# A graph network on one core: transfers with other outer row counts, and four accumulation tables instead of eight

## The chip, the cores and the metric

The kernel runs on one core of one Trainium2 chip. The metric is the device time of one execution in microseconds (us), the median of the runs shown. A core has five instruction streams: TensorE (PE, with its weight loads PEld), VectorE (DVE), ScalarE (ACT), GpSimd (POOL) and SyncE (SP), which here only issues transfers. 16 DMA engines move the data between HBM and the on-chip memory (SBUF).

## The reference

Two message-passing layers on a graph of 6250 nodes and 206250 directed edges, 128 features, float32. Both normalise first and add their result to `x`.

```
h = relu(layernorm(x))
# layer 0: graph convolution, with self loops added
deg  = segment_sum(w, src); dinv = rsqrt(deg)
x   += relu(segment_sum(dinv[src] * w * dinv[dst] * (h @ kernel)[dst], src) + bias)
h = relu(layernorm(x))
# layer 1: messages along each edge in both directions, mean over them
fwd  = concat([h[src], edge_attr]) @ W_fwd + b_fwd      # summed at dst
back = concat([h[dst], edge_attr]) @ W_back + b_back    # summed at src
agg  = (segment_sum(fwd, dst) + segment_sum(back, src)) / count
x   += gamma * layernorm(leaky_relu(agg) + h) + beta
```

The edges come sorted by `dst`.

## The kernel before

The program is a row of blocks, one after the other; between two blocks all engines meet. What matters of each:

**Setup** (`setup_and_degrees`, L86 to L368). SP loads `src`, `dst` and the weights as 128 partitions of 1616 edges. 206250 edges fill 127 such rows (`ROWFULL`), and one row has 1018. Then `x` comes in as 125 partitions (`NP`) of 50 nodes. DVE starts its own work when the three edge arrays are there (L248), turns them into tables of node rows and columns, and then makes one-hot tables for 101 steps of 16 times 128 edges, which PE multiplies into counts and degrees (L300 to L320, L354). Its last instruction (L337) scales `x` by the inverse root of the degree and lets SP store it as `g` (L186). Meanwhile SP stores the padded edge arrays (L166), loads them again in groups (L170), and makes `near` (L172): a table in HBM of `NEAR` = 51563 rows of 64 floats, row r being the 64 keys from edge 4r on. Next SP fills the accumulation tables with zeros (L178), ten transfers of 640 KB for each of the `K` = 8 tables. All these are queued on SP in the order of the code. The block ends when all of them have landed.

**Edge pass** (`edge_pass`, name `gw`). 202 groups of 8 times 128 edges. PE builds the message rows with one-hot matrices, ACT copies them to SBUF, and POOL adds each chunk of 128 rows to an HBM table with one indirect DMA (L497), table `j % K` for chunk `j` of the group. Ahead of a chunk POOL waits until the last add to the same table has landed (L495).

**Node update** (`gcn_nodes`). Nodes are again 125 partitions of 50. SP loads `g` and the left half of the columns of all `K` tables, in two halves of 25 nodes a partition (L710), into three buffers; DVE adds them up (L813). Queued behind the first three loads on SP is a small load of node counts (L721), which DVE needs (L769) to find rows of `near`; POOL then gathers 50 tiles of them (L744), and DVE (L801) turns them into the places that the next block uses. DVE's order is: the row numbers, the sum of half 0, its products (L820, L824), the places, the sum of half 1, its products. At the end SP stores `x1` and `h1`.

**Counts times features** (`dense_sums`). 25 steps (`t`), in each of which DVE makes one-hot tables (L1077, L1078), PE makes count matrices of them and multiplies them with the features, and ACT and DVE take the results away. Beside it POOL adds up the right half of the columns of the `K` tables (L1052), one half table in each of the steps 2 to 2K - 1.

**Last update** (`last_nodes`). Loads of `h1` and `x1` as 125 partitions (L1370, L1371), 50 small products with bias, activation and normalisation, and two stores of half the output (L1374).

Of the kernel before, what the change touches and what calls it, by code (L numbers as in the profile page):

```python
# [53 lines left out]
K = 8  # L54
# [6 lines left out]
NEAR = E // STEP + 1  # L61
# [5 lines left out]
ROUND = 12582912.0  # L67

# [21 lines left out]
def setup_and_degrees(nc, d):  # L90
# [4 lines left out]
    with ExitStack() as ctx:  # L95
# [58 lines left out]
        @block.sync  # L154
        def _(sp):

            sp.wait_ge(pads, 3)
            for a, t in ((d.src, src_i), (d.dst, dst_i), (d.w, w_run)):
                sp.dma_start(t[0:ROWFULL, :], a[0:ROWFULL * EC].rearrange("(p c) -> p c", c=EC)).then_inc(edges_in, 16)
                sp.dma_start(t[ROWFULL:ROWFULL + 1, 0:ROWTAIL], a[ROWFULL * EC:E].rearrange("(p c) -> p c", p=1)).then_inc(edges_in, 16)  # L160
            sp.dma_start(x[:], d.x.rearrange("(p t) f -> p t f", p=NP)).then_inc(x_in, 16)
# [24 lines left out]
            sp.dma_start(d.g[0:N, :].rearrange("(p t) f -> p t f", p=NP), x[:]).then_inc(stored, 16)  # L186
            sp.wait_ge(stored, 16 * 4)
            sp.wait_ge(cleared, 16 * (CUT * K + 2))
# [18 lines left out]
        def _(act):  # L207

            act.wait_ge(x_in, 16)
# [18 lines left out]
        def _(dve):  # L228
# [19 lines left out]
            dve.wait_ge(edges_in, 16 * 6)  # L248
# [399 lines left out]
def gcn_nodes(nc, d):  # L648
# [4 lines left out]
    with ExitStack() as ctx:  # L653
# [51 lines left out]
        def _(sp):  # L705
            def load_part(n):
                r, k = divmod(n, K)
                if n >= PB:
                    sp.wait_ge(part_used, n - PB + 1)
                sp.dma_start(part[:, n % PB, :, :], half(nodes(d.tab_gcn[k]), r)[:, :, 0:F]).then_inc(part_in[n % PB], 16)  # L710

            sp.dma_start(d.count_dst.rearrange("(p t) -> p t", p=NP), d.cnt_dst[:]).then_inc(cnt_stored, 16)
            for at, t in ((0, one), (1, next_one)):
                sp.dma_start(t[:], d.dst_f[at:at + E].rearrange("(p c) -> p c", p=NP)).then_inc(dst_in, 16)
            sp.dma_start(half(acc, 0), half(nodes(d.g), 0)).then_inc(acc_in[0], 16)
# [11 lines left out]
            sp.dma_start(x[:], nodes(d.x)).then_inc(x_in, 16)  # L727
            sp.dma_start(half(acc, 1), half(nodes(d.g), 1)).then_inc(acc_in[1], 16)
# [4 lines left out]
            sp.dma_start(nodes(d.x1), x[:]).then_inc(stored, 16)  # L733
            for r in range(2):
                sp.wait_ge(h_ready, HT * (r + 1))
                sp.dma_start(half(nodes(d.h1), r), half(acc, r)).then_inc(stored, 16)
            sp.wait_ge(stored, 16 * 4)
# [11 lines left out]
        def _(dve):  # L749
# [8 lines left out]
            def starts():  # L758
# [4 lines left out]
                dve.wait_ge(dst_in, 32)  # L763
# [45 lines left out]
            def add_up(r):  # L809
                dve.wait_ge(acc_in[r], 16)  # L810
                for n in range(r * K, (r + 1) * K):
                    dve.wait_ge(part_in[n % PB], 16 * (n // PB + 1))
# [20 lines left out]
            dve.wait_ge(x_in, 16)  # L833
# [85 lines left out]
def dense_sums(nc, d):  # L919
# [7 lines left out]
    with ExitStack() as ctx:  # L927
# [70 lines left out]
        def _(sp):  # L998
# [5 lines left out]
            def store(i, h, first, last):  # L1004
                t = 2 * i + h
                if isinstance(i, int) and i == 0:
                    sp.dma_start(d.src_attr_half(h), d.table_half(0, h)).then_inc(acc_in[h], 16)
                elif isinstance(i, int) and i < K:
                    if i >= 2:
                        sp.wait_ge(part_used, 2 * (i - 2) + h + 1)  # L1010
                    sp.dma_start(d.part_half(h), d.table_half(i, h)).then_inc(part_in[h], 16)
# [13 lines left out]
        def _(pool):  # L1025
# [10 lines left out]
            def take(i, h, first, last):  # L1036
# [10 lines left out]
                if isinstance(i, int) and 1 <= i < K:  # L1047
                    pool.wait_ge(acc_in[h], 16)
                    pool.wait_ge(part_in[h], 16 * i)
# [279 lines left out]
def last_nodes(nc, d):  # L1329
# [3 lines left out]
    with ExitStack() as ctx:  # L1333
# [30 lines left out]
        def _(sp):  # L1364
# [5 lines left out]
            sp.dma_start(h1[:], nodes(d.h1)).then_inc(h1_in, 16)  # L1370
            sp.dma_start(x1[:], nodes(d.x1)).then_inc(x1_in, 16)  # L1371
# [3 lines left out]
            sp.wait_ge(stored, 32)  # L1375

        @block.gpsimd
        def _(pool):

            pool.wait_ge(w_in, 16 * 8)  # L1380
            pool.wait_ge(x1_in, 16)
# [3 lines left out]
        def _(dve):  # L1385
# [17 lines left out]
            for r in range(2):  # L1403
                for t in range(r * HT, (r + 1) * HT):
# [8 lines left out]
                    if t == 0:  # L1413
                        dve.wait_ge(h1_in, 16)
# [157 lines left out]
```

## Time and profile before

| | |
|---|---|
| median of 3 runs | 6291.11 us (6288.08 to 6294.46) |
| profiled execution, its own time | 6287.51 us |
| its span in the trace | 6285.7 us |
| busy: PE, DVE, POOL, ACT | 57%, 48%, 48%, 30% of the span |
| bytes moved | 622.18 MB, 99 GB/s over the span |

No engine is busy for much more than half of the span, so the kernel has to be read block by block: setup from 0 to 1128.7 us, edge pass to 4390.4, node update to 4815, counts times features to about 6094, last update to the end. In the views below a time in brackets, as `[14.31 <-DMA ...]`, is how long the engine had stood idle before the instruction and what ended that. "DMA share" is how busy the 16 DMA engines are together: 0.06 is one engine at work all the time, 1.0 is all sixteen.

### The profile page before, as it was taken

The page shows a single profiled execution, that of the slowest core. Times are in us where ns is not written, and L with a number is a line of the kernel's source. Part 1 is how long each engine was busy: PE and PEld are TensorE (multiplying, and loading weights), DVE is VectorE, ACT ScalarE, POOL GpSimd, SP SyncE. Part 2 cuts the span into 40 slices and gives each one's busy share as a digit, 9 for nine tenths or more (in the row PEclk, how much of TensorE's full clock was granted, in tenths as well). Part 3 has the DMA queues.
Part 4 walks back from the last instruction along what each step waited for, and adds up shares of the span by engine and source line. Part 5 has one row for each costly group of instructions (what it writes and reads, how often), then busy time and mean ns, then how long its engine had stood idle before and what let it go on. Part 6 is the DMA issues. An engine that isn't in the chain of part 4 may idle for free. (4 is left out here: it accounts for less than half of the span.)

```text
span 6285.7 us, 93695 instructions
## 1 busy us (share of the span) xinstructions
PE 3579.1 (57%) x27946; PEld 3167.1 (50%) x28096; DVE 3009.3 (48%) x4263; ACT 1906.9 (30%) x5027; POOL 2993.7 (48%) x1727
## 2 busy tenths in 40 slices
PE   0555000566666666666666666664012988888984
PEld 0444000565666556665566555664011766666764
DVE  3999000444444444444444444443134656565536
ACT  1011000333333333333333333332013545455532
POOL 0000000688888888888888888887301011110000
PEclk9777555777777777777777777776555999999997
DMA  3300029677777777777777777776333111110011
GB/s 74 24 18 18 18 98 273 141 137 137 133 134 137 137 135 134 136 137 137 135 133 137 137 137 134 134 137 109 100 103 110 35 35 35 35 35 25 5 36 54
DMA packets 687907, 622.18 MB, mean 99 GB/s; under 512 B 252021, under 2 KB 595789, under 8 KB 685852
## 3 DMA queue, kind: packets, MB, share of 16 engines
q0 software_dynamic: 234304, 213.56, 28.8%
q1 hardware_dynamic: 453432, 406.13, 22.2%
q8 instruction: 133, 2.18, 0.1%
q14 instruction: 38, 0.31, 0.0%
HBM read 327.05 MB, written 305.66 MB: 101 GB/s over the span
## 5 line engine op out<-in xcount | busy, mean ns | idle before, releaser
L497 POOL DMA_INDIRECT gcn_sums<-gw_sums,gw_to_i x1616 | 2750.8, 1702 | 1490.3 <-ACT gw_sums L643 1003.5
L581 PE MATMUL bank<-gw_window,gw_spread_hot 128*128 128x128 f32 x3232 | 793.4, 349 | 1291.4 <-DVE gw_spread_hot L539 1290.4
L581 PEld LDWEIGHTS bank<-gw_window,gw_spread_hot 128*128 128x128 f32 x3232 | 642.5, 255 | 1329.0 <-issue 809.3
L643 ACT COPY gw_sums<-bank 128x256 f32<-128x256 f32 x1616 | 601.9, 372 | 1465.6 <-PE bank L606 1169.8
L600 PE MATMUL bank<-gw_sum_hot,gw_attrs 128*128 128x128 f32 x3232 | 795.4, 336 | 395.5 <-DVE gw_sum_hot L543 198.0
L633 ACT ACTIVATE gw_pay<-bank,gw_rec 128x128 f32<-128x128 f32 x1616 | 593.5, 370 | 1160.2 <-PE bank L581 1139.6
L600 PEld LDWEIGHTS bank<-gw_sum_hot,gw_attrs 128*128 128x128 f32 x3232 | 629.1, 242 | 444.3 <-issue 444.3
L604 PE MATMUL bank<-gw_pay,gw_same 128*128 128x128 f32 x3232 | 757.1, 323 | 2.7 <-ACT gw_pay L633 2.6
L561 DVE CAST gw_to_i<-gw_to_f 128x8 int32<-128x8 f32 x202 | 34.9, 173 | 1481.2 <-DMA gcn_sums<-gw_sums,gw_to_i 1481.1
L606 PE MATMUL bank<-gw_attrs,gw_same 128*128 128x128 f32 x3232 | 744.0, 318 | 0.0
L604 PEld LDWEIGHTS bank<-gw_pay,gw_same 128*128 128x128 f32 x3232 | 625.8, 241 | 3.6 <-ACT gw_pay L633 2.9
L606 PEld LDWEIGHTS bank<-gw_attrs,gw_same 128*128 128x128 f32 x3232 | 613.3, 236 | 0.0
L1154 PE MATMUL bank<-ds_counts,ds_parts 128*128 128x256 bf16 x3675 | 597.3, 278 | 0.0
L539 DVE TENSOR_SCALAR gw_spread_hot<-gw_rel_b,part 128x1024 f32<-128x1024 bf16 x202 | 230.4, 1141 | 532.1 <-DMA gw_rel_b<-dst_offset 504.5
L354 PE MATMUL bank<-places,row_hot 128*128 128x200 bf16 x1616 | 269.6, 293 | 339.6 <-DVE places L307 339.6
L1199 ACT COPY ds_turned<-bank 128x1024 bf16<-128x1024 bf16 (+1 forms) x325 | 311.5, 963 | 470.3 <-PE bank L1140 470.3
L1103 DVE TENSOR_TENSOR src_sums<-src_sums,bank 128x512 f32<-128x512 f32 (+1 forms) x325 | 211.3, 656 | 485.4 <-PE bank L1170 481.3
L1170 PE MATMUL bank<-ds_turned,ds_now 128*128 128x512 bf16 (+1 forms) x1800 | 435.0, 377 | 10.0 <-issue 2.8
L1052 POOL TENSOR_TENSOR src_attr<-src_attr,attr_by_dst 125x3200 f32<-125x3200 f32 x14 | 102.0, 7285 | 623.3 <-issue 519.7
L541 DVE TENSOR_TENSOR gw_same<-gw_key_b,gw_rec 128x1024 f32<-128x1024 int16 x202 | 397.2, 1966 | 0.0
L354 PEld LDWEIGHTS bank<-places,row_hot 128*128 128x128 bf16 x1616 | 195.2, 121 | 372.4 <-DVE places L307 360.4
L1183 ACT CAST ds_counts<-bank 128x392 bf16<-128x392 f32 x800 | 344.5, 502 | 122.4 <-PE bank L1120 122.0
(199 smaller groups left out, 4793.7 us busy)
## 6 DMA issues: line engine op xcount, KB each, us to landing
gw_attrs<-in_edge_attr SPq DMA_DIRECT2D x201, 512.0 KB
gw_rel_b<-dst_offset SPq DMA_DIRECT2D x202, 256.0 KB, 4.0
gw_key_b<-src_key SPq DMA_DIRECT2D x202, 256.0 KB
gcn_sums<-zeros SPq DMA_DIRECT2D x80, 640.0 KB
gcn_sums<-gw_sums,gw_to_i POOLq DMA_INDIRECT x1616, 3.8
n_part<-gcn_sums SPq DMA_DIRECT2D x16, 1562.5 KB
attr_by_dst<-gcn_sums SPq DMA_DIRECT2D x14, 1562.5 KB
gw_window<-g SPq DMA_DIRECT2D x202, 64.0 KB, 4.0
```

Of the source, the lines that this page charges most:

```text
L354: nc.tensor.matmul(hist[:, 0:4 * NT], row_hot[:, h, 0, j, :], col_w[:, h, j, :, :].rearrange("p s n -> p (s n)"), **ends)
L497: nc.gpsimd.indirect_dma_start(out=tables[j % K], out_offset=bass.IndirectOffsetOnAxis(ap=to_i[:, h, j:j + 1], axis=0), in_=sums[:, h, j, ...
L541: nc.vector.tensor_tensor(same[:, h, :, :], by_chunk(key_b), per_edge(key_row), ALU.is_equal).then_inc(same_ready, 1)
L581: nc.tensor.matmul(row_bank[j % 2][:, 0:F], spread_hot[:, h, j, :], window[:, h, :], start=True, stop=True).then_inc(row_ready, 1)
L600: nc.tensor.matmul(win_bank[h][:, 0:P], attrs[:, h, j, :], sum_hot[:, h, j, :], **ends)
L604: last = nc.tensor.matmul(bank[j % B][:, 0:F], same[:, h, j, :], pay[:, h, j, :], start=True, stop=True)
L606: last = nc.tensor.matmul(bank[j % B][:, F:2 * F], same[:, h, j, :], attrs[:, h, j, :], start=True, stop=True)
L633: nc.scalar.activation(pay[:, h, j, :], row, ACT.Copy, scale=rec[:, h, 3, j:j + 1]).then_inc(paid, 1)
L643: nc.scalar.copy(sums[:, h, j, :], bank[j % B][:, 0:width]).then_inc(staged, 1)
L1154: ins = nc.tensor.matmul(row_bank[:, 0:2 * P], parts[:, tile, s, :], counts[:, h, tile, :, :].rearrange("p b q -> p (b q)"), start=(tile = ...
L1170: ins = nc.tensor.matmul(back_bank[v][:, 0:n], now[:, h, half, s, :], turned[:, v, half, 0:n], start=(half == 0 and s == 0), stop=(half == ...
L1183: nc.scalar.copy(to, pair_bank[batch % B][:, 0:PB * HH].rearrange("p (c k) -> p k c", c=PB)).then_inc(pair_copied, 1)
```

## The change

The number of tables `K` goes from 8 to 4. Every transfer over 125 partitions in the places shown is cut into one of 120 and one of 5, and the three edge loads of 127 partitions into one of 112 and one of 15. `near` has 51568 rows instead of 51563, the next multiple of 16. The semaphore counts follow. (Broadcast loads of 125 partitions and the 128-partition transfers are as they were.)

```diff
-K = 8
+K = 4
-NEAR = E // STEP + 1
+NEAR = 16 * -(-(E // STEP + 1) // 16)
+NODE_CUTS = (slice(0, 120), slice(120, NP))
+EDGE_CUTS = (slice(0, 112), slice(112, ROWFULL))
...
-                sp.dma_start(t[0:ROWFULL, :], a[0:ROWFULL * EC].rearrange("(p c) -> p c", c=EC)).then_inc(edges_in, 16)
+                rows = a[0:ROWFULL * EC].rearrange("(p c) -> p c", c=EC)
+                for cut in EDGE_CUTS:
+                    sp.dma_start(t[cut, :], rows[cut, :]).then_inc(edges_in, 16)
...
-            sp.dma_start(d.g[0:N, :].rearrange("(p t) f -> p t f", p=NP), x[:]).then_inc(stored, 16)
+            for cut in NODE_CUTS:
+                sp.dma_start(d.g[0:N, :].rearrange("(p t) f -> p t f", p=NP)[cut], x[cut]).then_inc(stored, 16)
...
-                sp.dma_start(part[:, n % PB, :, :], half(nodes(d.tab_gcn[k]), r)[:, :, 0:F]).then_inc(part_in[n % PB], 16)
+                for cut in NODE_CUTS:
+                    sp.dma_start(part[cut, n % PB, :, :], half(nodes(d.tab_gcn[k]), r)[cut, :, 0:F]).then_inc(part_in[n % PB], 16)
...
-            sp.dma_start(h1[:], nodes(d.h1)).then_inc(h1_in, 16)
+            for cut in NODE_CUTS:
+                sp.dma_start(h1[cut], nodes(d.h1)[cut]).then_inc(h1_in, 16)
...
-                sp.dma_start(half(nodes(d.out), 1 - r), half(agg, 1 - r)).then_inc(stored, 16)
+                for cut in NODE_CUTS:
+                    sp.dma_start(half(nodes(d.out), 1 - r)[cut], half(agg, 1 - r)[cut]).then_inc(stored, 16)
```

The same cut stands at the loads of `x` (twice), the two key arrays `one` and `next_one`, `g` (both halves), the half tables in `dense_sums`, and `x1`, and at the stores of `x1` and `h1`.

On SP, in setup before, from the last padded array's reload to the end of the block's transfers, with the number of rows behind each:

```order
L170 DMA rec<-w_pad 128x202x8
L172 DMA near<-src_float 51563x64
L178 DMA gcn_sums<-zeros 128x1280 [waits setup_zeroed]
L178 DMA gcn_sums<-zeros 128x1280 x79
L180 DMA g<-zeros 75x256
L180 DMA h<-zeros 75x256
L183 DMA dst_offset<-rel 128x202x8 [waits setup_rec_ready]
L184 DMA edge_records<-rec 128x202x32
L186 DMA g<-x_sb 125x6400 [waits setup_g_ready]
```

And in the changed kernel, whose lines are numbered a little higher:

```order
L175 DMA rec<-w_pad 128x202x8
L177 DMA near<-src_float 51568x64
L183 DMA gcn_sums<-zeros 128x1280 [waits setup_zeroed]
L183 DMA gcn_sums<-zeros 128x1280 x39
L185 DMA g<-zeros 75x256
L185 DMA h<-zeros 75x256
L188 DMA dst_offset<-rel 128x202x8 [waits setup_rec_ready]
L189 DMA edge_records<-rec 128x202x32
L192 DMA g<-x_sb 120x6400 [waits setup_g_ready]
L192 DMA g<-x_sb 5x6400
```

The order is the same; 40 of the 80 fills are gone, and the store of `g` is two transfers.

On POOL, in the edge pass's loop, the first five indirect adds of a group before. The names of the waits are those of the first block that used the semaphore: `setup_normed` is here ACT's "chunk is in SBUF", `setup_g_ready` the group's row numbers, and `setup_step`, `setup_stored`, `setup_cleared` and `gw_added3`, `gw_added4` the landing of adds to tables 0, 1, 2, 3 and 4:

```order
L493 ISA [waits setup_g_ready]
L495 REGISTER_ALU [waits setup_normed]
L497 DMA gcn_sums<-gw_sums,gw_to_i 6400x256 [waits setup_step]
L493 REGISTER_ALU
L497 DMA gcn_sums<-gw_sums,gw_to_i 6400x256 [waits setup_normed,setup_stored]
L493 REGISTER_ALU
L497 DMA gcn_sums<-gw_sums,gw_to_i 6400x256 [waits setup_normed,setup_cleared]
L493 REGISTER_ALU
L497 DMA gcn_sums<-gw_sums,gw_to_i 6400x256 [waits setup_normed,gw_added3]
L493 REGISTER_ALU
L497 DMA gcn_sums<-gw_sums,gw_to_i 6400x256 [waits setup_normed,gw_added4]
```

The same five in the changed kernel:

```order
L499 ISA [waits setup_g_ready]
L501 ISA [waits setup_normed]
L503 DMA gcn_sums<-gw_sums,gw_to_i 6400x256 [waits setup_step]
L499 REGISTER_ALU
L503 DMA gcn_sums<-gw_sums,gw_to_i 6400x256 [waits setup_normed,setup_stored]
L499 REGISTER_ALU
L503 DMA gcn_sums<-gw_sums,gw_to_i 6400x256 [waits setup_normed,setup_cleared]
L499 REGISTER_ALU
L503 DMA gcn_sums<-gw_sums,gw_to_i 6400x256 [waits setup_normed,gw_added3]
L499 REGISTER_ALU
L501 ISA [waits setup_normed]
L503 DMA gcn_sums<-gw_sums,gw_to_i 6400x256 [waits setup_step]
```

The fifth add goes to table 0 again and waits for the first add of the same group, four adds back, where before each waited for the one eight back. One register instruction more stands in each group.

On SP, at the start of the node update before (the wait ahead of L721 is for the store of the counts):

```order
L712 DMA count_dst<-cnt_dst 125x50
L714 DMA n_one<-dst_float 125x1650
L714 DMA n_next_one<-dst_float 125x1650
L715 DMA n_acc<-g 125x3200
L710 DMA n_part<-gcn_sums 125x25x128 x3
L721 DMA n_cnt_tp<-count_dst 48x128 [waits setup_hot_used,setup_mean_ready]
L722 DMA n_cnt_tp<-count_dst 1x106
L710 DMA n_part<-gcn_sums 125x25x128 [waits setup_runs_ready] x5
L725 DMA n_w<-in_L_gnn_kernel 128x128
L726 DMA n_bias<-in_L_gnn_bias 125x128
L727 DMA n_x<-in_x 125x6400
```

In the changed kernel, from the third half table on:

```order
L717 DMA n_part<-gcn_sums 120x25x128
L717 DMA n_part<-gcn_sums 5x25x128
L730 DMA n_cnt_tp<-count_dst 48x128 [waits setup_hot_used,setup_mean_ready]
L731 DMA n_cnt_tp<-count_dst 1x106
L717 DMA n_part<-gcn_sums 120x25x128 [waits setup_runs_ready]
L717 DMA n_part<-gcn_sums 5x25x128
L734 DMA n_w<-in_L_gnn_kernel 128x128
L735 DMA n_bias<-in_L_gnn_bias 125x128
L737 DMA n_x<-in_x 120x6400
L737 DMA n_x<-in_x 5x6400
```

One half table instead of five stands between the counts and `x`.

## Rows read from the trace of the kernel before

**Rows 1.** Windows of setup: us, busy us (instructions) of each engine, TensorE clock, DMA share, GB/s.
```profile
20.00:30.00 10.00, 0.00 (x0) 0.00 (x0) 0.00 (x0) 0.00 (x0) 0.00 (x0) 1.00 0.06 27
200.00:300.00 100.00, 56.67 (x680) 49.67 (x678) 100.00 (x150) 0.00 (x0) 0.00 (x0) 0.77 0.08 18
930.00:940.00 10.00, 0.00 (x0) 0.00 (x0) 0.00 (x0) 0.00 (x0) 0.00 (x0) 0.50 1.02 411
1115.00:1120.00 5.00, 0.00 (x0) 0.00 (x0) 0.00 (x0) 0.00 (x0) 0.00 (x0) 0.50 0.30 128
```

**Rows 2.** Timeline of SP's issues in setup and at the edge pass's start: start, us.
```profile
168.22 14.96 SPq L172 DMA_DIRECT2D near<-src_float  x1
183.22 840.77 SPq L178 DMA_DIRECT2D gcn_sums<-zeros  x80
...
1078.90 22.60 SPq L186 DMA_DIRECT2D g<-x_sb  x1
1128.68 0.38 SPq L448 DMA_DIRECT2D gw_rec<-edge_records  x1
```

**Rows 3.** Timeline of DVE in setup: its first conversion and its last instruction.
```profile
102.69 1.00 DVE L249 CAST attr_sums<-src_i 128x1616 f32<-128x1616 int32 x1 [99.30 <-DMA attr_sums<-in_edge_weight]
623.63 6.82 DVE L337 TENSOR_TENSOR x_sb<-x_sb,dinv 125x6400 f32<-125x6400 f32 x1
```

**Rows 4.** The indirect adds of L497 in the edge pass.
```profile
L497 POOL DMA_INDIRECT gcn_sums<-gw_sums,gw_to_i x1616: 1543/1547/2832, 1141.0 to 4383.1; - x180
...
DMA to landing us min/median/max: 3.6/3.8/7.9
```

**Rows 5.** Timeline of POOL there, the first add of a group.
```profile
2006.66 1.55 POOL L497 DMA_INDIRECT gcn_sums<-gw_sums,gw_to_i  x1 [0.30 <-DMA gcn_sums<-gw_sums,gw_to_i]
```

**Rows 6.** Timeline of SP: node update's first and last issues, next block's first.
```profile
4390.44 0.26 SPq L712 DMA_DIRECT2D count_dst<-cnt_dst  x1
...
4784.63 9.86 SPq L736 DMA_DIRECT2D h<-n_acc  x2
4815.22 7.56 SPq L1001 DMA_DIRECT2D src_sums<-h  x5
```

**Rows 7.** Timeline of DVE in the node update.
```profile
4470.64 0.28 DVE L769 TENSOR_REDUCE n_tile_cnt<-n_cnt_tp 50x1 f32<-50x128 f32 x1 [58.93 <-DMA n_cnt_tp<-count_dst]
4476.09 10.54 DVE L813 TENSOR_TENSOR n_acc<-n_acc,n_part 125x3200 f32<-125x3200 f32 x3
...
4595.85 0.35 DVE L820 SCALAR_TENSOR_TENSOR n_scaled<-bank,dinv,n_bias 125x128 f32<-125x128 f32 x1 [21.68 <-DMA n_x<-in_x]
...
4743.06 3.49 DVE L813 TENSOR_TENSOR n_acc<-n_acc,n_part 125x3200 f32<-125x3200 f32 x1 [13.37 <-DMA n_part<-gcn_sums]
```

**Rows 8.** Timeline of POOL there: the first, second and last of 50 gathers.
```profile
4474.99 1.01 POOL L744 DMA_INDIRECT n_near<-near,n_near_row_i  x1 [90.30 <-POOLq L742]
4476.30 4.13 POOL L744 DMA_INDIRECT n_near<-near,n_near_row_i  x1 [0.30 <-issue]
...
4551.58 0.94 POOL L744 DMA_INDIRECT n_near<-near,n_near_row_i  x1 [0.30 <-issue]
```

**Rows 9.** POOL's adds of half tables, L1052, all 14.
```profile
L1052 POOL TENSOR_TENSOR src_attr<-src_attr,attr_by_dst x14: 6959/7134/7875, 4976.1 to 5652.5; 125x3200 f32<-125x3200 f32 x14
```

**Rows 10.** Timeline of POOL: one add, and two copies of later steps.
```profile
5444.34 7.76 POOL L1052 TENSOR_TENSOR src_attr<-src_attr,attr_by_dst 125x3200 f32<-125x3200 f32 x1 [44.27 <-issue]
...
5735.93 0.83 POOL L1046 COPY ds_now<-ds_parts 128x768 bf16 x1 [52.48 <-PE bank L1170]
...
6009.99 0.83 POOL L1046 COPY ds_now<-ds_parts 128x768 bf16<-128x768 bf16 x1 [47.57 <-PE bank L1170]
```

**Rows 11.** Timeline of DVE beside that add.
```profile
5445.22 7.71 DVE L1078 TENSOR_TENSOR ds_hi_hot<-ds_numbers,ds_twos 128x1568 bf16<-128x1568 bf16 x1
```

**Rows 12.** Timeline of DVE in the last update: first use of `h1`, last instruction.
```profile
6146.14 0.35 DVE L1415 SCALAR_TENSOR_TENSOR n_agg<-n_leaky,n_per_count,n_h 125x128 f32<-125x128 f32 x1 [22.51 <-DMA n_h<-h]
...
6262.45 3.49 DVE L1437 TENSOR_TENSOR n_agg<-n_agg,n_x 125x3200 f32<-125x3200 f32 x1
```

More of the change, by code:

```diff
@@ L207, in _ @@
         def _(act):
-            act.wait_ge(x_in, 16)
+            act.wait_ge(x_in, 32)
             for t in range(NT):
@@ L709, in load_part @@
                     sp.wait_ge(part_used, n - PB + 1)
-                sp.dma_start(part[:, n % PB, :, :], half(nodes(d.tab_gcn[k]), r)[:, :, 0:F]).then_inc(part_in[n % PB], 16)
+                for cut in NODE_CUTS:
+                    sp.dma_start(part[cut, n % PB, :, :], half(nodes(d.tab_gcn[k]), r)[cut, :, 0:F]).then_inc(part_in[n % PB], 16)
             sp.dma_start(d.count_dst.rearrange("(p t) -> p t", p=NP), d.cnt_dst[:]).then_inc(cnt_stored, 16)
             for at, t in ((0, one), (1, next_one)):
-                sp.dma_start(t[:], d.dst_f[at:at + E].rearrange("(p c) -> p c", p=NP)).then_inc(dst_in, 16)
-            sp.dma_start(half(acc, 0), half(nodes(d.g), 0)).then_inc(acc_in[0], 16)
+                for cut in NODE_CUTS:
+                    sp.dma_start(t[cut, :], d.dst_f[at:at + E].rearrange("(p c) -> p c", p=NP)[cut, :]).then_inc(dst_in, 16)
+            for cut in NODE_CUTS:
+                sp.dma_start(half(acc, 0)[cut], half(nodes(d.g), 0)[cut]).then_inc(acc_in[0], 16)
             for n in range(PB):
@@ L726, in _ @@
             sp.dma_start(bias[:], d.bias.rearrange("(o f) -> o f", o=1).to_broadcast([NP, F])).then_inc(w_in, 16)
-            sp.dma_start(x[:], nodes(d.x)).then_inc(x_in, 16)
-            sp.dma_start(half(acc, 1), half(nodes(d.g), 1)).then_inc(acc_in[1], 16)
+            for cut in NODE_CUTS:
+                sp.dma_start(x[cut], nodes(d.x)[cut]).then_inc(x_in, 16)
+            for cut in NODE_CUTS:
+                sp.dma_start(half(acc, 1)[cut], half(nodes(d.g), 1)[cut]).then_inc(acc_in[1], 16)
             for n in range(K, 2 * K):
@@ L732, in _ @@
             sp.wait_ge(x1_ready, NT)
-            sp.dma_start(nodes(d.x1), x[:]).then_inc(stored, 16)
+            for cut in NODE_CUTS:
+                sp.dma_start(nodes(d.x1)[cut], x[cut]).then_inc(stored, 16)
             for r in range(2):
                 sp.wait_ge(h_ready, HT * (r + 1))
-                sp.dma_start(half(nodes(d.h1), r), half(acc, r)).then_inc(stored, 16)
-            sp.wait_ge(stored, 16 * 4)
+                for cut in NODE_CUTS:
+                    sp.dma_start(half(nodes(d.h1), r)[cut], half(acc, r)[cut]).then_inc(stored, 16)
+            sp.wait_ge(stored, 16 * 7)
         @block.gpsimd
@@ L832, in _ @@
             dve.wait_ge(w_in, 32)
-            dve.wait_ge(x_in, 16)
+            dve.wait_ge(x_in, 32)
             products(0)
@@ L1006, in store @@
                 if isinstance(i, int) and i == 0:
-                    sp.dma_start(d.src_attr_half(h), d.table_half(0, h)).then_inc(acc_in[h], 16)
+                    for cut in NODE_CUTS:
+                        sp.dma_start(d.src_attr_half(h)[cut], d.table_half(0, h)[cut]).then_inc(acc_in[h], 16)
                 elif isinstance(i, int) and i < K:
@@ L1010, in store @@
                         sp.wait_ge(part_used, 2 * (i - 2) + h + 1)
-                    sp.dma_start(d.part_half(h), d.table_half(i, h)).then_inc(part_in[h], 16)
+                    for cut in NODE_CUTS:
+                        sp.dma_start(d.part_half(h)[cut], d.table_half(i, h)[cut]).then_inc(part_in[h], 16)
                 elif isinstance(i, int) and i == K and h == 0:
@@ L1047, in take @@
                 if isinstance(i, int) and 1 <= i < K:
-                    pool.wait_ge(acc_in[h], 16)
-                    pool.wait_ge(part_in[h], 16 * i)
+                    pool.wait_ge(acc_in[h], 32)
+                    pool.wait_ge(part_in[h], 32 * i)
                     if i >= 2:
@@ L1369, in _ @@
             sp.dma_start(row_sums[:], d.row_t[:, 0:N]).then_inc(row_in, 16)
-            sp.dma_start(h1[:], nodes(d.h1)).then_inc(h1_in, 16)
-            sp.dma_start(x1[:], nodes(d.x1)).then_inc(x1_in, 16)
+            for cut in NODE_CUTS:
+                sp.dma_start(h1[cut], nodes(d.h1)[cut]).then_inc(h1_in, 16)
+            for cut in NODE_CUTS:
+                sp.dma_start(x1[cut], nodes(d.x1)[cut]).then_inc(x1_in, 16)
             for r in range(2):
                 sp.wait_ge(out_ready, r + 1)
-                sp.dma_start(half(nodes(d.out), 1 - r), half(agg, 1 - r)).then_inc(stored, 16)
-            sp.wait_ge(stored, 32)
+                for cut in NODE_CUTS:
+                    sp.dma_start(half(nodes(d.out), 1 - r)[cut], half(agg, 1 - r)[cut]).then_inc(stored, 16)
+            sp.wait_ge(stored, 64)
         @block.gpsimd
```

16 lines of the change are left out of this document (8 added, 8 removed).

## The prediction

> **What bounds the kernel now.** I read the windows of setup first, then SP's timeline, then DVE's and POOL's, block by block.
>
> The windows show how many DMA engines a transfer uses [rows 1]. With the 127-row edge loads alone in flight the share is 0.06 and the rate 27 GB/s: one engine of 16. The 125-row store of `g` has 0.30 and 128 GB/s, five engines at 25.6. The 128-row fills have 1.02 and 411 GB/s, sixteen at 25.7. From 200 to 300 us there are 18 GB/s at 0.08 (one engine, and a little for bookkeeping): that is `near`, in 256-byte pieces. 127 is prime, 125 has 5, 128 has 16, and 51563 has no divisor from 2 to 16. So the count that decides is the largest divisor up to 16 of the outer rows.
>
> Four places pay for it. Setup: DVE idles 99.3 us for the edges, then works until 630.45 [rows 3]; `near` holds the queue, the fills behind it take until about 1040, two small stores and `g` follow, and the edge pass starts at 1128.68 [rows 2]. Node update: DVE waits for half tables, `x` and the counts [rows 7]. The last update waits for `h1` [rows 12] and for its stores. The edge pass is another matter: 1616 indirect adds in 3242 us from first to last start are 2.006 us each, of which the add is 1.55 or more and a gap 0.30 [rows 4, 5]; POOL is never still, so it sets the pace there.
>
> **Edge loads.** The three arrays are 2.46 MB, by one engine at 26 GB/s 95 us. With 112 + 15 rows the most loaded engine has 8 rows of 6464 bytes and the tail, 56 KB for each array, 167 KB, 6.4 us. 102.69 was 2.8 (first issue) + 94 of data + 6 of rest, so DVE starts near 15.4: **-87**. DVE's 527.8 us from there to its end are its own work (100.00 of 100 us busy from 200 to 300 [rows 1]), so they only move: 630.45 becomes 543.
>
> **`near`, fills, small stores.** Sixteen engines at 18 GB/s copy 13.2 MB in 46 us; on one engine it stays 733. Issue comes at 168 - 87 = 81. Half the fills, 26.2 MB at 411 GB/s, are 64 us, and the small stores at most 55 (from the last fill's issue, 183.22 + 840.77 = 1024, to 1078.90 [rows 2]). Together 165 us, over by about 246; DVE works until 543. So the cover left is some 300 us: `near` could take 340 us and cost nothing. Without DVE's cover this part would cost the 165. The halved fills are worth nothing by themselves.
>
> **Store of `g`.** From the end of its issue, 1101.5, to 1128.68 are 27.2 us [rows 2], 25 of them data. Fifteen engines have 8 rows, five of them one more: 9 of 25.6 KB at 25.6 GB/s are 9 us. With a second issue 12 us. The edge pass starts at 543 + 12 = 555 instead of 1128.7: **-574** for setup.
>
> **Edge pass.** An add now waits for the one four back, started 8.0 us before; landing takes 3.8 us in the middle and 7.9 at most [rows 4]. So it costs nothing: below that it could only gain if fewer tables made an add faster, for which no row speaks. The extra register instruction per group: before a group's first add two more stand than before the others, and its gap is the same 0.30 [rows 5]. Bounds 0 and 0.06 us x 202 = 12 us; I take 0. 3261.7 us as before, and the node update starts at 3817.
>
> **Node update**, counted from its first issue; before, 424.8 us [rows 6]. A half table takes 13.37 + 3.49 = 16.9 us on five engines [rows 7], where each moves 625 pieces of 512 bytes, 27 ns a piece; now the fullest moves 225, **6.1 us**. The bounds are 6.1 and 16.9.
> - Keys 4.5, `g` 4.4, three half tables 18.3, start and landing 4.3: the counts come at 31.5, not 80.2.
> - DVE's row numbers take 4.35 until POOL's first gather [rows 7, 8]: 35.9. The 50 gathers took 77.5 us, 1.25 each and more beside one of DVE's adds (4.13 against 0.94 [rows 8]). 6 adds gave 15 us; now 4 adds and 3 similar operations fall there, 17.5: 80 us, and 3.6 landing: 119.5. **POOL's gathers are next to be late**; they were hidden.
> - Meanwhile DVE: three adds to 47.5, the fourth to 53, `x` (9 us instead of 25) at 59, products to 75, three operations for the places to 85, then a wait of 34 us for the gathers.
> - The places end 12.5 later, 132. Four adds, the last waiting for its buffer, to 147.6; ACT is then still busy with squares of half 0, for which I allow 2 us: 149.5.
> - From the last add's end, 4746.55, the block took 68.7 us [rows 6, 7]. Of these 20.7 stand behind the issue of the last store of `h1` (4794.49), which queues behind 4.8 MB more on the same five engines. With its own 4.4 us of data, 9.2 are left: 57.2. Sum 206.7: **-218**.
>
> **Counts times features.** While POOL adds (7.76 us), a DVE operation that lasts 0.97 elsewhere takes 7.71 [rows 10, 11], and PE then waits for its one-hots. A step with an add is (5652.5 - 4976.1) / 13 = 52.0 us [rows 9]; without one (6009.99 - 5735.93) / 6 = 45.7 [rows 10]. Eight adds fewer (14 to 6) at 6.3: **-50**. The bounds are 0, and 8 x 7.8 = 62.
>
> The Trainium skill (SBUF — State Buffer, Who interferes with whom) says that a VectorE instruction with two SBUF inputs and a GpSimd one that reads SBUF block each other fully. By that rule each add costs at most its own length, 8 x 7.1 = 57; by the steps of the trace it is 50. The trace agrees.
>
> **Last update.** `h1` on five engines is 24.4 us of data, on fifteen 8.8: -16. POOL's addition to `x1` and its collision with DVE stay. The two stores run from 6259 to the end; after DVE's end at 6265.94 [rows 12] 19.8 us are left, now 4.4 of data and 3 of start and end: -12. **-28**.
>
> **Sum.** 574 + 218 + 50 + 28 = 870. The profiled execution had 6287.5 (span 6285.7), 3.6 under the median 6291.1; so 5417 on its scale, and **5420** as a median.
>
> **The rivals.**
>
> *The scatter chain becomes the bound.* Two adds to one table are now four apart. If an add had to wait, the step is a quarter of the landing time. For it: the largest landing seen, 7.9 us, is only 0.1 under 8.0. Against: the middle is 3.8. At 8.5 us it costs 0.12 x 1616 = 190 and gives 5610. The sum of 870 is used up at (2.006 + 0.54) x 4 = 10.2 us landing; above that, at 10.7, the time is 6490 and the kernel slower. Chance 4%, and 1% for slower.
>
> *`near` stays on one engine* (if the copy's other side decides). It then starts at 81, ends at 814, fills to 878, small stores to 933, `g` to 945, 390 later than 555: 5810. Against it: the 128-row fills do use all. 3%.
>
> *The cut pieces do not run wider.* The Trainium skill (DMA: Bandwidth & Descriptors, Rules for kernel authors) advises against two transfers for two parts of the partitions, since both go through the same sixteen engines anyway. As a mechanism of this kernel: the edge loads keep 87, `g` 14, the last update 28, and the half tables stay at 16.9 us, so that the counts come at 80 and the node update takes about 277, 71 more. 5420 + 87 + 14 + 28 + 71 = 5620. Against it: the whole transfers of 127 and 125 rows used one and five engines [rows 1], so there is something to widen. The same page (Why a DMA increments its semaphore by 16 and not by 1) says that the largest divisor up to 16 decides. 5%.
>
> *Only a smaller thing is off*: instruction delivery, the gathers, clock, 30 to 70 us either way, inside the range.
>
> **How the numbers follow.** Forecast 86%, scatter chain 5%, `near` 3%, no wider 5%, other 1%. The range is made of the forecast's own terms: below, 50 us if gathers and half tables run freer than I take them and the adds cost 62; above, 12 for the register instruction, 1% of the edge pass (33), and 25 for the node update: 5370 to 5490. Within 0.2%, or 12.6 us of 6291, a measurement tells nothing from no change; faster 0.98, same 0.005, slower 0.015.
>
> **What the changed profile would show.** DVE's first conversion near 15 us; DMA share near 1 while `near` is copied, and no stretch at 18 GB/s; the edge pass starting at 555, with an add every 2.006 us and gaps of 0.30; the counts about 31 us after the node update's first issue, then DVE idle some 34 us until the gathers have landed; 6 adds of L1067, and long operations at the line of the one-hots only beside them; `h1` 16 us earlier. Wrong it would be by gaps on POOL that end with the landing of an add, by a window of 18 GB/s, or by half tables 17 us apart.

## The result

The changed kernel took 5476.8 us (median, 5471.4 to 5481.0), the kernel before 6290.6 beside it: 0.8706, 95% interval 0.8694 to 0.8718. The forecast was 5420, range 5370 to 5490. The time lies in the range and 57 us above the forecast. The profiled execution took 5479.9 (span 5478.1), and its forecast was 5417. The blocks, each from its first DMA issue to the next block's, divide the span and so nearly all of the difference.

| block, us | before | forecast | changed |
|---|---|---|---|
| setup | 1128.7 | 555 | 565.2 |
| edge pass | 3261.8 | 3262 | 3277.4 |
| node update | 424.8 | 207 | 226.1 |
| counts times features | 1281.9 | 1232 | 1227.7 |
| last update | 188.6 | 161 | 181.6 |

SP's issues in setup and at the edge pass's start, in the timeline of the changed kernel (start, us):

```profile
76.03 14.25 SPq L177 DMA_DIRECT2D near<-src_float  x1
90.33 101.27 SPq L183 DMA_DIRECT2D gcn_sums<-zeros  x40
...
543.03 0.70 SPq L192 DMA_DIRECT2D g<-x_sb  x2
565.20 0.37 SPq L454 DMA_DIRECT2D gw_rec<-edge_records  x1
```

`near` and the 40 fills are issued by 192 us, in place of 1024 [rows 2], and their data are through by about 207; no stretch at 18 GB/s and a share of 0.08 is left. DVE's last instruction of setup ends at 543.0, as forecast, and sets the store of `g`. But from there the edge pass is 22.2 us away, not 12. The windows of the changed kernel (columns as in [rows 1]) say why:

```profile
120.00:140.00 20.00, 12.44 (x152) 10.92 (x148) 20.00 (x30) 0.00 (x0) 0.00 (x0) 0.74 1.18 262
205.00:220.00 15.00, 8.01 (x110) 7.15 (x107) 15.00 (x24) 0.00 (x0) 0.00 (x0) 0.86 0.13 47
545.00:547.00 2.00, 0.00 (x0) 0.00 (x0) 0.00 (x0) 0.00 (x0) 0.00 (x0) 0.50 0.94 205
3864.00:3868.00 4.00, 0.00 (x0) 0.00 (x0) 0.00 (x0) 0.00 (x0) 0.00 (x0) 0.50 1.12 183
```

The first row is the copy of `near`. The third is `g`'s 120 rows. The share of 0.94 is the fifteen engines that the reshaping was to give, yet they move 205 GB/s, 13.7 each, where five moved 25.6 each and sixteen 25.7 [rows 1]. The fourth row is the half tables of the node update: all engines busy, 183 GB/s. **A share near 1 isn't a rate near the top; the last column has to be read beside it.**

The edge pass, by its line (least, middle and longest ns; first and last start), and two places of POOL's timeline:

```profile
L503 POOL DMA_INDIRECT gcn_sums<-gw_sums,gw_to_i x1616: 1542/1547/3742, 577.5 to 3833.1; - x180
```
```profile
639.60 1.54 POOL L503 DMA_INDIRECT gcn_sums<-gw_sums,gw_to_i  x1 [0.30 <-issue]
641.96 1.55 POOL L503 DMA_INDIRECT gcn_sums<-gw_sums,gw_to_i  x1 [0.82 <-DMA gcn_sums<-gw_sums,gw_to_i]
```

First to last start is 3255.6 us, against 3242.1 [rows 4]. The second add waited 0.82 us for an earlier add to land. Of the 1615 gaps 29 are over 0.335 us, and they hold 11.2 us more than 0.30 each would; before there was none. The semaphore times of the trace say when each add landed: in 25 of the 29 the late add starts 0.76 to 0.78 us after the landing of the one four back, and no add of the pass starts sooner than 0.76 after it. 24 of the 29 are the seventh add of a group, which waits for the third.

DVE and POOL in the node update, in the timeline of the changed kernel:

```profile
3889.80 0.28 DVE L782 TENSOR_REDUCE n_tile_cnt<-n_cnt_tp 50x1 f32<-50x128 f32 x1 [31.90 <-DMA n_cnt_tp<-count_dst]
...
3977.07 1.83 DVE L814 TENSOR_SCALAR n_hi<-n_near 128x3200 f32<-128x3200 f32 x1 [16.81 <-DMA n_near<-near,n_near_row_i]
...
4005.28 3.49 DVE L826 TENSOR_TENSOR n_acc<-n_acc,n_part 125x3200 f32<-125x3200 f32 x1 [5.16 <-DMA n_part<-gcn_sums]
```
```profile
3894.16 1.01 POOL L757 DMA_INDIRECT n_near<-near,n_near_row_i  x1 [59.49 <-DVE n_near_row_i L792]
```

Counted from the block's first issue at 3842.64, the counts are there at 47.2 (forecast 31.5), the gathers have landed at 134.4 (119.5), the last add starts at 162.6. The late counts carry 16 of the block's 19 us: from the counts to the landed gathers it is 87.2 us, forecast 88.0. What comes after is 91.7, forecast 87.2; 3.5 of those 4.5 us are the last add, which waited 5.16 us for its half table; the forecast had 1.6 for it.

Counts times features has six adds of half tables, as forecast, and each is a little shorter than before (6.96 us in the middle, 7.13 in [rows 9]):

```profile
L1067 POOL TENSOR_TENSOR src_attr<-src_attr,attr_by_dst x6: 6959/6962/6967, 4222.8 to 4483.6; 125x3200 f32<-125x3200 f32 x6
```

The last update, in the timelines of PE (the first product with `row_sums`) and DVE (first use of `h1`, last instruction); the block begins at 5296.46:

```profile
5331.40 0.80 PE L1477 MATMUL bank<-n_w,n_row_sums 128*125 128x128 f32 x2 [13.51 <-DMA n_row_sums<-row_sums_t]
```
```profile
5347.39 0.35 DVE L1433 SCALAR_TENSOR_TENSOR n_agg<-n_leaky,n_per_count,n_h 125x128 f32<-125x128 f32 x1 [13.57 <-DMA n_h<-h]
...
5464.08 3.49 DVE L1455 TENSOR_TENSOR n_agg<-n_agg,n_x 125x3200 f32<-125x3200 f32 x1
```

`h1` is first used 50.9 us after the block's start, against 49.0 before [rows 12]; it was to come 16 us earlier. From DVE's end, 5467.57, to the span's end are 10.5 us, in place of 19.8: the stores did become shorter, by 9.3 of the forecast 12.

### The profile page after: what moved, and what is told of

It reads as the page before. It is cut to its first block and busy times, and to the rows that moved or that the text cites. A ratio compares the mean times of both kernels' runs of the same rounds, so it can differ in the third digit from the quotient of the medians.

```text
span 5478.1 us, 93494 instructions
## 1 busy us (share of the span) xinstructions
PE 3562.1 (65%) x27946; PEld 3159.2 (58%) x28096; DVE 2931.5 (54%) x4255; ACT 1898.5 (35%) x5027; POOL 2932.3 (54%) x1719
## 5 line engine op out<-in xcount | busy, mean ns | idle before, releaser
L1061 POOL COPY ds_now<-ds_parts 128x768 bf16 (+1 forms) x25 | 28.0, 1119 | 770.9 <-PE bank L1185 770.9
L1135 PE MATMUL bank<-ds_hi_hot,ds_lo_hot 128*128 128x98 bf16 x3200 | 282.7, 214 | 101.6 <-DVE ds_hi_hot L1093 101.6
```

## The experiments

A ratio is to the kernel before, timed on the same chip; a time without one is one execution.

**The terms one by one.**

*near_only*: the kernel before with a round row count for `near` alone.
```diff
-NEAR = E // STEP + 1
+NEAR = 16 * -(-(E // STEP + 1) // 16)
```

> The kernel before with 51568 rows in near and nothing else. If the copy then runs on all engines and DVE's work covers it with the fills and small stores, the edge pass starts at DVE's end plus the five-engine store of g, 630 + 27 = 658 instead of 1129, and the time is about 5820. If the copy stays on one engine, no change: 6290. In the changed kernel the fills and near overlapped and the whole queue was empty by about 207, so I expect the first. Edge pass, node update and last update as before.

Measured 5824.2 us; setup 659.0, the other blocks as before to within 5 us. `near` alone is 466 of the 814 us gained.

*k4_only*: the kernel before with four tables.
```diff
-K = 8
+K = 4
```

> The kernel before with four tables and nothing else. If the prediction's terms are separable: half the fills stand behind the one-engine copy of near, so setup loses 64 us (26.2 MB at 411 GB/s); the half tables stay at 16.9 us each but are half as many, the counts still come at 80 us, the node update falls from 425 to about 280; the steps with a POOL add fall from 14 to 6, -52; the last update stays. Sum 6030. What it is to tell: whether the edge pass is longer with four tables (3277 us as in the changed kernel, against 3262) with everything else as before. If four tables are the cause, 3275 or more here and a time near 6043; if the earlier start or the other transfers are, 3262.

Measured 6068.4 us. Setup 1064.5 (half the fills, with `near` still in front of them), node update 292.2 (with 21 us of pauses that are told of under x1_later), counts times features 1227.6 (-54); but the edge pass 3282.4 in place of 3261.8, and the last update, in which nothing differs, 199.8 in place of 188.6.

*all_but_k*: the changed kernel with eight tables.
```diff
-K = 4
+K = 8
```

> The changed kernel with eight tables again. If four tables cost the edge pass some 13 us (a few gaps on POOL above 0.30), it falls from 3277 to about 3262 here; if not, it stays. Node update: four more half tables on each side, of which the second half's adds (4 x 3.5) and the wait for their buffers show, about +30; the steps with an add go from 6 to 14, +52. Time about 5545 with the first, 5560 with the second.

Measured 5579.6 us (5576.7 to 5587.7), ratio 0.8869 [0.8854, 0.8884], 103 more than the changed kernel. Setup is the same, 564.9: the fills are hidden at either number. Node update 294.5, counts times features 1271.7, edge pass 3265.0. So four tables are worth 68 and 44 us in two blocks and cost 12 in a third. The adds of the edge pass by their line, with eight tables:

```profile
L503 POOL DMA_INDIRECT gcn_sums<-gw_sums,gw_to_i x1616: 1544/1548/3869, 576.9 to 3822.8; - x180
```

3245.9 us from first to last start. With eight tables the edge pass took 3261.8 to 3265.8 in three kernels, with four 3277.4 to 3290.3 in ten. No kernel of one kind reaches into the other: **the four tables cost the edge pass 12 to 29 us**. Long gaps there are none in the three, and 29 to 52 in each of the ten.

*k2*: the changed kernel with two tables, the loads of later half tables begun where the first three end.
```diff
-K = 4
+K = 2
```
```diff
-            for n in range(K, 2 * K):
+            for n in range(max(K, PB), 2 * K):
```

> The changed kernel with two tables: an add waits for the one two back, started 4.0 us before. Shown so far is 3.8 us from issue to landing, but not whether the issue is counted from the instruction's start or from its end, 1.55 us later. Counted from the start, a table's cycle is 3.8 + 0.3 = 4.1 us, 2.05 for an add, and the edge pass is some 70 us longer; with 26 us less in the steps with POOL adds and some 15 less in the node update the time is about 5505. Counted from the end, the cycle is 1.55 + 3.8 + 0.3 = 5.65, 2.83 for an add, the edge pass about 4570 us long, and the time about 6730. The second would also put the limit of four tables nearer: 5.65 of 8.0 us.

Measured 6377.6 us, slower than the kernel before; the edge pass takes 4186.9. The adds by their line:

```profile
L503 POOL DMA_INDIRECT gcn_sums<-gw_sums,gw_to_i x1616: 1542/1546/3806, 580.0 to 4746.3; - x180
```

The add itself is as long as ever (1546 ns), but an add starts only every 4166.3 / 1615 = 2.58 us, and two to one table 5.16 apart. That is the mean round trip of an add on one table. By the semaphore times, of which this trace lacks some, 1254 of 1614 adds start 0.76 to 0.80 us after the landing of the one before on their table, and a landing takes at least 4.3 us on average from the add's start. The 3.8 of [rows 4] was too short, because that line of the view counts 808 of the 1616 adds only: the tables 0, 5, 6 and 7, for whose landings the records are complete. By all semaphore times of the kernel before, the adds to table 2 take 6.2 us in the middle and 8.5 at the longest. The rival's mechanism exists; at four tables the room is 8.0 us on average against 5.16.

**The halved rate.** The store of `g` was half as fast as its engines. One theory: what counts is where the rows lie that the engines move at the same moment, and 15 engines with 8 rows each are a bad pattern. The other: something shared, or the number 15, limits any such transfer.

*cut112*:
```diff
-NODE_CUTS = (slice(0, 120), slice(120, NP))
+NODE_CUTS = (slice(0, 112), slice(112, NP))
```

> The changed kernel with the node rows cut into 112 + 13 instead of 120 + 5. In the changed kernel the 120-row transfers kept fifteen engines busy (share 0.90 to 0.96) at only 192 to 205 GB/s, 13 GB/s each, where five engines had 25.6 each. Theory A (where the rows lie): fifteen engines of eight neighbouring rows meet at the same part of SBUF and each runs at half speed; seven rows each on sixteen engines lie staggered, and the edge loads, cut so, had up to 290. Then g needs some 11 us of data instead of 18, the counts come near 38 instead of 47, and the time falls by 20 to 40 to about 5447. Theory B (a limit of the path to HBM for such rows, whatever the cut): still 200 GB/s and 5477. Theory C (the second, small piece is what costs, since it comes after the first): thirteen rows on thirteen engines instead of five on five, nearly the same, 5475.

Measured 5468.4 us (5465.1 to 5472.9), ratio 0.8683 [0.8668, 0.8697]. Two windows of `g`'s store, and one of the half tables:

```profile
550.00:552.00 2.00, 0.00 (x0) 0.00 (x0) 0.00 (x0) 0.00 (x0) 0.00 (x0) 0.50 1.11 371
...
554.00:556.00 2.00, 0.00 (x0) 0.00 (x0) 0.00 (x0) 0.00 (x0) 0.00 (x0) 0.50 1.12 397
```
```profile
3864.00:3868.00 4.00, 0.00 (x0) 0.00 (x0) 0.00 (x0) 0.00 (x0) 0.00 (x0) 0.50 1.18 203
```

`g` goes at 371 to 397 GB/s, and from its issue to the edge pass are 14.8 us in place of 22.2: a shared limit of 205 is out. The half tables, in pieces of 512 bytes, stay near 200: for them the cut changes little. Node update 215.3, counts times features 1217.5.

*cut105*: again fifteen engines, with seven rows each.
```diff
-NODE_CUTS = (slice(0, 120), slice(120, NP))
+NODE_CUTS = (slice(0, 105), slice(105, NP))
```

> The changed kernel with the node rows cut in 105 and 20 instead of 120 and 5: again 15 engines for the large piece, but 7 rows for each in place of 8. Changed kernel: the store of g runs at 205 GB/s and lasts 17.5 us (543.0 to about 560.5); cut in 112 and 13 (16 engines, 7 rows each) it ran at 371 to 397 GB/s. Theory A (what halves the rate is where the rows lie that the engines move at one moment, eight rows apart): 7 rows apart are as good with 15 engines as with 16, so 340 to 375 GB/s and a store of about 11 us. Theory B (15 engines are slower than 16, whatever the rows): 190 to 215 GB/s as with 120 rows.

Two windows of `g`'s store:

```profile
554.00:556.00 2.00, 0.00 (x0) 0.00 (x0) 0.00 (x0) 0.00 (x0) 0.00 (x0) 0.50 0.94 371
556.00:558.00 2.00, 0.00 (x0) 0.00 (x0) 0.00 (x0) 0.00 (x0) 0.00 (x0) 0.50 0.97 346
```

The same share as with 120 rows, and 346 to 371 GB/s in place of 205 (320 and 243 in the two windows before, the second with a share of 0.70). **So it isn't that there are fifteen engines, but how the rows are dealt to them.** Eight rows to each of fifteen is the slow pattern. Eight rows to an engine can't be all of it: 128 rows are eight to each of sixteen, and they ran at 411 GB/s [rows 1]. (The whole took 5488.1, with pauses in the node update as under x1_later.) An estimate by it, 8 ports at the 25.6 GB/s of one engine, is 205, and the trace agrees with it to the digit. That is an argument and not shown: the runs show the rates of the row patterns, not the ports, and sixteen engines at rows 0, 8, 16 would use 8 ports too, so the 411 GB/s of 128 rows need them to be dealt in another way, which no run here shows.

*rows128*: `g`'s halves, the half tables of the node update and `h1` loaded as one transfer of 128 whole rows each.
```diff
-            for cut in NODE_CUTS:
-                sp.dma_start(half(acc, 0)[cut], half(nodes(d.g), 0)[cut]).then_inc(acc_in[0], 16)
+            sp.dma_start(half(acc_all, 0), half(whole_rows(d.g), 0)).then_inc(acc_in[0], 16)
```

> The changed kernel, with g, the half tables of the node update and h1 loaded as 128 rows of 50 nodes in one transfer each (the tables have 6400 rows; the last three are loaded and not used). Theory A (where the rows lie): these come at 25 GB/s an engine; a half table's 200 pieces of 512 bytes an engine at 27 ns are 5.4 us, the counts come at about 32 us and not 47, the node update loses 15 to 20 us, and the last update's first use of h1 comes near 33 us after its first issue and not 51. Together about -30, 5445. Theory B: loads from HBM stay near 200 GB/s, counts at 45, 5475.

Measured 5477.9 us (5475.3 to 5480.9), ratio 0.8694 [0.8679, 0.8708]. Two windows in the node update, the first of `g`'s half and the second of a half table:

```profile
3864.00:3868.00 4.00, 0.00 (x0) 0.00 (x0) 2.85 (x2) 0.00 (x0) 0.00 (x0) 0.50 0.98 356
3872.00:3876.00 4.00, 0.00 (x0) 0.00 (x0) 0.00 (x0) 0.00 (x0) 0.00 (x0) 0.50 1.21 291
```

`g`'s half, in pieces of 12.8 KB, goes at 356 GB/s. The half tables go at 291 in place of 183, 18 an engine, near the 19 of the prediction's 512 bytes in 27 ns. The counts are there at 32.5 us, near the forecast's 31.5, and the node update takes 209.4 (forecast 206.7). So in the node update the forecast failed by the rates alone. The last update does not gain: 184.0, `h1` at 53.0.

**The waits.**

*counts_first*: the loads of the counts ahead of the keys, `g` and the half tables in SP's order.
```diff
+            sp.wait_ge(cnt_stored, 16)
+            sp.wait_ge(zeroed, 1)
+            sp.dma_start(cnt_tp[0:whole, :], ...).then_inc(cnt_in, 16)
             for at, t in ((0, one), (1, next_one)):
```

> The changed kernel with the loads of the node counts moved ahead of keys, g and half tables on SP. In the changed kernel the counts come 47 us after the block's start and DVE later waits 16.8 us for POOL's gathers. If the gathers are what is late, they now start about 20 us after the block's start (after the keys, which DVE takes first), 32 earlier, are over before DVE asks, and the 16.8 us go: 5460. If the half tables or x bound the block, nothing: 5477.

Measured 5470.9 us (5466.8 to 5476.6), ratio 0.8683 [0.8669, 0.8698]. The first gather waits 32.0 us for DVE's row numbers in place of 59.5, and the node update takes 205.0, 21 less. POOL's chain from the counts on is what this block waits for.

*x1_later*: in the last update SP waits for `h1` before it issues `x1`.
```diff
+            sp.wait_ge(h1_in, 32)
             for cut in NODE_CUTS:
                 sp.dma_start(x1[cut], nodes(d.x1)[cut]).then_inc(x1_in, 16)
```

> The changed kernel, but in the last update SyncE waits until h1 has landed before it issues x1, which only the very last addition needs, some 100 us later. Changed kernel: h1 is first used 50.9 us after that block's first issue, row_sums 34.9, the block takes 181.6. Theory A (x1 takes its share of the DMA engines although it was issued behind the other two; 8.65 MB had moved when h1 landed, 6.83 without x1): h1 at 38 to 41, row_sums at 27 to 31, the block 169 to 172, the whole 11 us less, 0.8690 of the kernel before in place of 0.8706 or a little under. Theory B (the engines work their rings in order, x1 moves behind h1 anyway): h1 at 51, nothing changes.

Measured 5502.5 us (5497.2 to 5508.4), ratio 0.8738 [0.8723, 0.8752]: slower than the changed kernel as it was first timed, though not clear of its repetition below. In the last update the edit did what it was to do, in part: `row_sums` at 34.0 us, `h1` at 44.0 in place of 50.9, the block 174.6 in place of 181.6. The loss is elsewhere, in a node update of 243.0 (226.1) and counts times features of 1237.5 (1227.7), whose code is the same. (The latter took 1224 and 1234 in the two repetitions below, so 10 us of it are within what it does by itself.) DVE's timeline in the node update:

```profile
3940.55 0.35 DVE L833 SCALAR_TENSOR_TENSOR n_scaled<-bank,dinv,n_bias 125x128 f32<-125x128 f32 x1 [18.71 <-DMA n_x<-in_x]
...
3950.93 0.35 DVE L833 SCALAR_TENSOR_TENSOR n_scaled<-bank,dinv,n_bias 125x128 f32<-125x128 f32 x1 [4.94 <-issue]
```

From 3940.6 to 3978.3 DVE begins 11 tiles and pauses six times, 30.9 us in all; in the changed kernel a tile takes 0.6 to 0.8 us. PE, ACT and DVE take turns in this loop. The last pause ends 6 us after the last of the gathers, which run beside them at their usual 1.25 us.

*all_three*: cut112, rows128 and counts_first together.

> The changed kernel with three edits at once: the node rows cut in 112 and 13, the half tables, g's halves and h1 loaded as whole 128 rows, the loads of the counts ahead of them. Alone they gave 0.8683, 0.8694 and 0.8683 of the kernel before (0.8706 without them). Theory A (they shorten different waits: the node update 215.3, 209.4 and 205.1 us in place of 226.1, and counts by features 10 us through the cut): node update 185 to 195, the whole 0.8640 to 0.8655. Theory B (they take the same wait twice, the node update does not go under 203): 0.8670 to 0.8680.

Measured 5451.1 us (5450.2 to 5455.0), ratio **0.8658 [0.8644, 0.8673]**, the best of all kernels and under the changed one's interval. Counts times features 1214.4, last update 176.9; the node update is 207.7, no better than with one edit, because it has pauses of 3.5 to 7.7 us at the tiles as well, five of them, 31 us. The expected saving of that block was not seen.

*again* and *one_wait_more*: the changed kernel unaltered, and with one wait that costs nothing.
```diff
+            sp.wait_ge(w_in, 16 * 8)
             for r in range(2):
                 sp.wait_ge(out_ready, r + 1)
```

> The changed kernel once more, unaltered, beside the next one on one chip. With x1 held back the last update took 174.6 us in place of 181.6, but the node update before it, in which nothing differs, 243.0 in place of 226.1: between 3945.3 and 3978.3 DVE, ScalarE and TensorE went through seven tiles of the node update one every 3 to 8 us, in place of one in 0.6 to 0.8. Cut in 105 and 20, and with all three edits, the same stretch shows it too. Theory A (it belongs to a program, from how its code happens to lie or to its timing): the unaltered kernel again has none, node update 224 to 230, ratio 0.869 to 0.872. Theory B (it comes and goes with the chip or the hour): the unaltered kernel has it now as well, node update 240 to 245, ratio 0.873 to 0.875.

> The changed kernel with one more wait in SyncE's part of the last update (for the weights, which have landed 100 us before), so that its code is one instruction longer and nothing else moves. Theory A (how the code lies sets whether the slow tiles appear): the node update may be 240 to 245 and the ratio 0.873 to 0.875, with the last update at 181 to 182. Theory B (they come with the chip or the hour): as the unaltered kernel beside it, to 0.2%.

Measured 5486.4 us (5475.7 to 5496.3), ratio 0.8722 [0.8701, 0.8742], and 5488.9 (5484.1 to 5500.7), 0.8722 [0.8707, 0.8737]. Neither has a pause: node update 227.0 and 227.6. One instruction more does not bring them; that says nothing against the other theory, since this pair ran on another chip than x1_later. Where the loop runs beside the gathers, the kernels divide by chip: cut105, x1_later and all_three on one, k4_only and k2 on another all have pauses (21 to 51 us in all); cut112, rows128 and counts_first on a third, these two on a fourth and the changed kernel have none. In the kernel before, near_only and all_but_k the loop begins when the gathers are over, and they can't tell. That speaks for the chip or the hour, but no kernel in which the two run beside each other was profiled on chips of both kinds, so it **stays open**. It also says how far the small comparisons carry: the unaltered kernel came to 0.8706 once and to 0.8722 once. The gains of cut112, rows128 and counts_first alone, 0.8683 to 0.8694, rest on the lengths of their blocks more than on their ratios; only the three together stand clear.

## Why the prediction was right, and where it was off

**Setup (forecast 555, measured 565.2).** The edges' 87 us, the hidden `near` and the hidden fills came as worked out: DVE's first conversion is at 15.3 (15.4), its end at 543.0. The step that was mis-sized is "9 of 25.6 KB at 25.6 GB/s are 9 us", 12 with the second issue: it was 22.2, since an engine with eight neighbouring rows moved 13.7 GB/s. Cut in 112 the same bytes went at up to 397 GB/s, and the 22.2 became 14.8. The rival "`near` stays on one engine" is out by near_only, whose setup fell to 659.0.

**Edge pass (0, measured +16).** The failing step is "an add now waits for the one four back, started 8.0 us before". 8.0 is the mean distance, and "7.9 at most" was read from half of the adds. The wait is not met by the landing alone: the next add starts 0.76 us after it at the earliest. The third add of a group lands after 6.2 us in the middle, 8.5 at the longest, and the add four behind it, when it does not have to wait, starts 8.4 us or more after it as a rule. In the changed kernel landings of up to 7.7 us delayed no such add, and those from 7.75 on did. For the add at 641.96 it was 8.23 + 0.77 = 8.99 us. So the rival of the scatter chain was right in its mechanism and had its threshold wrong: the wait begins where one add's landing and the 0.76 reach the distance of that place in the group, long before the mean landing reaches the mean distance. (Its time for 10.7 us of landing is 6500 by its own terms, not 6490.) It stayed small because few landings are long. The kernels with eight and with four tables show the sign beyond doubt; of the 12 to 29 us the gaps hold 11.2 in the changed kernel and 11 to 19 in the ten. The register instruction was rightly taken as nothing: the common gap stayed 0.30.

**Node update (-218, measured -199).** The order of the waits came as forecast, with POOL's gathers next to be late and 79.4 us long (80). What failed is the size of the data terms ahead of the counts. "The fullest moves 225, **6.1 us**" for a half table was 8.7 us at 183 GB/s, 8 us over for three of them; the keys and `g`, put at 4.5 and 4.4 us, took about 16 together, 7 over. The counts came 16 late. rows128 gives the rate of the forecast (291 GB/s, counts at 32.5), and with it the block of the forecast. Why 512-byte pieces in 112 rows stay at 200 GB/s, where `g`'s long ones double, no run shows.

**Counts times features (-50, measured -54).** Right, and four tables alone give the same 54 in k4_only.

**Last update (-28, measured -7).** The stores gave 9.3 of 12. The failing step is "`h1` on five engines is 24.4 us of data, on fifteen 8.8: -16": it counts `h1` alone. Before, `h1` and `x1` had five engines each and left the rest to `row_sums`; now all three transfers are wide, `row_sums` came 10.9 us later than before (34.9 in place of 24.0) and `h1` no earlier. x1_later shows that `x1` has 7 us of it; that the rest is `h1` and `row_sums` sharing engines is argued. The row pattern is not the cause here: with 112 rows `h1` came at 53.3, with 128 at 53.0. In all of these kernels the last 10 us before `h1` run at some 100 GB/s and a share near 0.3, on a few engines; which ones, and why they are behind, is open. The 188.6 of the kernel before is also a low mark: with the same code in this block near_only took 193.3 and k4_only 199.8, with `h1` at 53.3 and 59.3.

**The whole.** Four of the five blocks came out longer than forecast, and the sum stayed in the range by some luck: the range had no term for the store of `g` (10 us over) or for the last update (21 over), and they were paid for by the 12, 33 and 25 us set aside for the edge pass and the node update, which used 15 and 19.

The rival "no wider" is refuted for such counts, and the advice of the Trainium skill (DMA: Bandwidth & Descriptors, Rules for kernel authors) against two transfers for two parts of the partitions does not hold for them: all_but_k differs from near_only by the edge loads and the cuts alone, and it is 245 us faster, 94 of them in setup and 130 in the node update.

## What to carry to other kernels

Give the outer rows of a transfer a large divisor up to 16, but read GB/s beside the share of engines: fifteen engines with eight rows each did half of what 112 rows on sixteen, or 105 on fifteen, did. When buffers are taken in turns, compare the longest landing, and the 0.76 us until the next use can start, with the distance of those two uses, place by place in the loop, not middle with mean; and look how many of the transfers a landing time in a view counts. A transfer that is made wider takes engines from those in flight beside it, so its gain is that of the whole group of transfers up to the first use, not its own.

## What the runs showed of the hardware

- 120 rows on fifteen engines: 205 GB/s at a share of 0.94; 105 rows on fifteen 346 to 371 at 0.94 to 0.97; 112 rows on sixteen 371 to 397 at 1.1; all with rows of 25.6 KB. 128 rows on sixteen: 411 with rows of 5 KB (the fills), 356 with rows of 12.8 KB (`g`'s half in rows128).
- Pieces of 512 bytes: 291 GB/s from 128 whole rows, 183 from 120, about 200 from 112.
- Indirect adds to one table in turn have a round trip of 5.16 us on average, measured as the distance of two such adds when only two tables are used. An add that waits for a landing starts 0.76 us after it, in all ten kernels with four tables and in k2.
- The landing of such an add depends on its place in the group: in the kernel before, 3.8 us in the middle for the first add of a group, 5.3, 6.2, 5.7 and 4.3 for the next four, 3.8 for the last three. Why is open.
- In five kernels (k4_only, k2, cut105, x1_later, all_three) the loop over the node update's tiles paused for up to 7.8 us at a time while POOL's gathers ran beside it, and no pause ended more than 8 us after the last of them; in the changed kernel and its repetition the same loop ran beside the same gathers without a pause. What sets it off is open.
